# A two-layer transformer kernel on one core: the second half of a decayed attention by way of a state, and a causal mask moved from the matrix engine to the vector engine

## The reference

```
# first attention: 16 heads of 128, 4 key/value heads, rotary, no softmax
lam  = 2 ** (-8 * (1..16) / 16)
o[i] = sum over j <= i of  exp(-lam * (i - j)) * (q[i] . k[j]) * v[j]
# second attention: 32 heads of 16, 8 key/value heads, rotary
scores = q @ k.T / sqrt(16) + triu(-inf, k=1);  y = softmax(scores) @ v
```

## Time and profile before

| | |
|---|---|
| median of 3 runs | 4115.63 us (4114.98 to 4118.08) |
| profiled execution, own time | 4116.67 us |
| its span, first to last instruction | 4114.9 us |
| mean granted TensorE clock | 0.967 of 2.4 GHz |
| PE, DVE, ACT, POOL busy | 3815.0, 2393.4, 1449.7, 1332.2 us |

### The profile page before, as it was taken

How to read it: one execution, slowest core, us unless ns; L and a number is a source line. 1 busy time by engine, 2 the same in 40 slices (tenths; PEclk the granted TensorE clock), 3 DMA queues, 4 the chain that set the end, 5 groups by cost and what they waited for, 6 DMA issues and landing times. The chain is left out here.

```text
span 4114.9 us, 51894 instructions
## 1 busy us (share of the span) xinstructions
PE 3815.0 (93%) x19048; PEld 2746.2 (67%) x19048; DVE 2393.4 (58%) x3950; ACT 1449.7 (35%) x2205; POOL 1332.2 (32%) x1674
## 2 busy tenths in 40 slices
PE   6877999999999999999999999999999999978678
PEld 5755777677767776677767776677767776664423
DVE  5644556555654666556654666456654665465347
ACT  4422342424243433424242433334242433314124
POOL 2421452235312541235313541244213541121114
PEclk9989999999999999999999999999999999987789
DMA  6456533254424433254324533354324433332304
GB/s 234 171 186 245 189 133 139 83 196 158 144 68 179 164 133 127 86 215 147 129 88 154 181 116 135 105 202 138 123 98 180 164 126 105 113 105 73 133 12 153
DMA packets 173802, 579.03 MB, mean 141 GB/s; under 512 B 14728, under 2 KB 14984, under 8 KB 168175
## 3 DMA queue, kind: packets, MB, share of 16 engines
q1 hardware_dynamic: 169854, 568.37, 38.8%
q10 hardware_dynamic: 3696, 7.34, 0.5%
HBM read 490.19 MB, written 84.93 MB: 140 GB/s over the span
## 5 line engine op out<-in xcount | busy, mean ns | idle before, releaser
L1776 PE MATMUL ps_P<-XnT_hi,w_ring 128*128 128x512 f32 x3328 | 1079.6, 406 | 51.6 <-DVE silu L1445 25.7
L1776 PEld LDWEIGHTS ps_P<-XnT_hi,w_ring 128*128 128x128 f32 x3328 | 610.0, 191 | 215.2 <-issue 76.2
L1776 PE MATMUL ps_P<-XnT_lo,w_ring 128*128 128x512 f32 x1664 | 659.0, 396 | 0.0
L1435 DVE TENSOR_REDUCE row_max<-ps_T 128x2 fp32r<-128x768 f32 (+3 forms) x448 | 399.3, 915 | 248.8 <-PE ps_T L1932 238.7
L833 POOL TENSOR_TENSOR pT_lo<-pf,pT_hi 128x512 fp32r<-128x512 f32 x320 | 410.8, 1291 | 303.7 <-ACT pT_hi L971 299.2
L1085 ACT ACTIVATE probs<-ps_E 128x1024 f32<-128x1024 f32 x320 | 327.1, 1022 | 393.2 <-PE ps_E L1947 393.2
L909 POOL TENSOR_TENSOR hT_lo<-hf,hT_hi 128x512 fp32r<-128x512 f32 x128 | 164.3, 1284 | 921.1 <-ACT hT_hi L971 921.1
L851 POOL TENSOR_SCALAR_AFFINE_SELECT probs<-probs 128x512 f32<-128x512 f32 x256 | 159.5, 635 | 652.1 <-ACT probs L1085 651.1
L1776 PEld LDWEIGHTS ps_P<-XnT_lo,w_ring 128*128 128x128 f32 x1664 | 317.6, 191 | 71.4
L1776 PE MATMUL ps_Y<-w_big,hT_hi 128*128 128x512 f32 x896 | 331.5, 416 | 23.0 <-POOL hT_lo L909 11.0
L824 POOL TENSOR_TENSOR sines<-swapped,sinT 128x512 f32<-128x512 f32 x160 | 213.2, 1332 | 348.7 <-ACT swapped L971 342.8
(11 more groups left out here) (307 smaller groups left out, 7263.5 us busy)
## 6 DMA issues: line engine op xcount, KB each, us to landing
w_ring<-split_dram SPq DMA_DIRECT2D x412, 512.0 KB, 3.4
w_big<-split_dram SPq DMA_DIRECT2D x64, 2048.0 KB, 7.8
dec<-decay SPq DMA_DIRECT2D x32, 1024.0 KB, 4.9
split_dram<-w_ring SPq DMA_DIRECT2D x58, 512.0 KB, 4.3
split_dram<-w_big SPq DMA_DIRECT2D x36, 512.0 KB, 4.4
wo1w<-split_dram SPq DMA_DIRECT2D x8, 2048.0 KB, 7.5
gatew<-split_dram SPq DMA_DIRECT2D x7, 2048.0 KB, 10.9
x_dram<-X SPq DMA_DIRECT2D x8, 1024.0 KB, 5.4
```

The source lines that it names most:

```text
L1435: last = dve.reduce_max(row_max[:, g % 2, block, heads_of(ns)].rearrange("p (b n) -> p b n", n=len(ns)), psT[:, :, at:at + len(ns) * w].re ...
L1776: last = pe.matmul(dst, stat[s_], mov[m_], start=first_ and k == 0, stop=last_ and k == n - 1)
```

## The change

In the first attention the sequence is cut in two halves of 256 tokens. Within each half, scores are made as before (three jobs of 512 columns in place of three blocks; the whole square between first and second half is gone). What the first half gives to the second goes by way of a state: keys are turned back to rows (`keys_back`, 4 matmuls of 128 columns), values of the first half are multiplied by their decay (DVE), `state` = keys x these values (6 matmuls of 512 columns), and `state_product` = state x queries of the second half (12 matmuls of 256 columns); DVE multiplies by a decay and adds it to the values' product of the second half. The ring has 10 jobs of ACT and POOL as before, but two of them are now the halves of `oT`. DVE's and ACT's order in the blocks is new.

`keys_back` writes bank Y0, which ACT empties after `swap` of the last unit and `rope_high` of the one before it; the same bank is the target of `output` 0 (and, for g = 0, of `all_values` 0).

In the second attention the two mask matmuls of each `scores` are left out. DVE adds the mask to the corner of the T banks, in place, and waits for its own sum before it takes the maxima. The copies `QT` (second half) and `yT` go from DVE to ACT. The weight pieces of pass 0 are staged in other buffers and split at other places of the blocks.

```diff
+P_F = {k: n for n, k in enumerate((0, 1, 2, 3, 4, 5, "state", 6, 7, 8, 9, "sum0", "sum1"))}
+P_HI = {k: n for n, k in enumerate((0, 1, 2, 3, "state", 4, 5, 6, 7, 8, 9))}
+UNIT_AT, KEYS_AT = (0, 1, 2, 3, 5), 4
@@ POOL blocks: 8 jobs pT_lo, then two that write oT_lo of the second half
@@ ACT rope
+                act.wait_ge(*proj.need(n, g, KEYS_AT))
+                copy(kv[0][:, :], ps["Y0"][:, :]).then_inc(*rope_hi.hit(n, g, KEYS_AT))
                 rope_high(n, g, NU - 1)
@@ ACT blocks
+                for k in range(NJOB):
+                    if k == 4:
+                        act.wait_ge(*pv.need(n, g, 1))
+                        copy(kv[0][:, :], ps[PB[g % 2]][:, :]).then_inc(*p_hi.hit(n, g, P_HI["state"]))
+                    if k == 6 and g == 0:
+                        values_high(n, 2)
+                        values_high(n, 3)
+                    if k == 7:
...
+                        act.wait_ge(*pv.need(n, g, 4))
+                        for h in range(2):
+                            copy(oT[0][:, 2 * h:2 * h + 2, 0:2 * P], ps[EB[h]][:, :]...)
+                    (then copy pT_hi for k < 8, oT_hi of the second half for k = 8, 9)
@@ ACT, second attention
-                copy(QT[:, g % 3, 0, :], ps[bank][:, :]).then_inc(*QT0_done.hit(c, g))
+                for pair, done in enumerate((QT0_done, QT1_done)):
+                    act.wait_ge(*pack.need(c, g, pair))
+                    copy(QT[:, g % 3, pair, :], ps[banks[pair]][:, :]).then_inc(*done.hit(c, g))
+                    copy(yT[:, g % 2, :], ps["O"][:, :]).then_inc(*yT_done.hit(c, g))
@@ DVE blocks
+                for k in range(2):
+                    if g == 0:
+                        values_low(n, k)
+                    scaled_values(n, g, k)
+                if g:
+                    accumulate(n, g - 1, 0)
+                    accumulate(n, g - 1, 1)
+                dve.wait_ge(*dec_in.need(n, g))
+                for k in range(2, 6):
+                    scaled_scores(n, g, k)
+                    if g == 1 and n:
+                        measure_pc(n - 1, k - 2)
+                dve.wait_ge(*p_hi.need(n, g, P_HI["state"]))
+                low(kv[1][:, :], ps[PB[g % 2]][:, :], kv[0][:, :])
+                (accumulate or values_low 2, 3; scaled_scores 6, 7; oT_lo of the first half, twice;
+                 scaled_scores 8, 9; for each half of the heads, after pv 7: pf = ps_E + pf)
@@ DVE, second attention
-                dve.tensor_copy(QT[:, g % 3, 1, :], ps[bank][:, :]).then_inc(*QT1_done.hit(c, g))
-                    dve.tensor_copy(yT[:, g % 2, :], ps["O"][:, :]).then_inc(*yT_done.hit(c, g))
+                    dve.tensor_tensor(corner, corner, mask[:, :]..., ALU.add).then_inc(*corner_done.hit(c, g, x_))
+                    dve.wait_ge(*corner_done.need(c, g, x_))
@@ PE
+            def keys_back(n, g):          # called after project(n, g, 3)
+                pe.wait_ge(*rope_lo.need(n, g, 0))
+                dst = fill("Y0", rope_hi.need(n, g, KEYS_AT))
+                for t in range(2):
+                    for s_ in range(2):
+                        last = pe.matmul(dst[:, cols(2 * t + s_)], kT[s_][:, cols(t)], identr[:, :], start=True, stop=True)
+            def blocks(n, g):
+                for k in range(2, 6):
+                    score_product(n, g, k)
+                if g == 0:
+                    all_values(n, 2)
+                state(n, g)
+                if g == 0:
+                    all_values(n, 3)
+                else:
+                    output(n, g - 1, 2)
+                    output(n, g - 1, 3)
+                value_product(n, g, 2)
+                value_product(n, g, 3)
+                score_product(n, g, 6)
+                score_product(n, g, 7)
+                value_product(n, g, 4)
+                for k in INTER:           # 8, 9
+                    state_product(n, g, k)
+                for k in range(5, 8):
+                    value_product(n, g, k)
@@ PE scores
-                for q in range(2):
-                    last = pe.matmul(corner..., ident_b[:, :], mask[:, :]..., start=False, stop=True)
```

More of the change, by code:

```diff
@@ L61 @@
 RAW = 4
-WO_AT = {2: 2, 5: 3}
 PHASES = [("pre", 0, "T"), ("pre", 0, "agg")]
@@ L175 @@
 assert len(PIECES) == NUNITS == len(set(PIECES))
+MOVED = sum(len(at) for key, at in FIRST.items() if key[0] != "slot")
 INDEX = {p: r for r, p in enumerate(PIECES)}
@@ L1054, in layout_high @@
+                        copy(oT[0][:, 2 * h:2 * h + 2, 2 * P:4 * P], pf[:, k % 2, :].rearrange("p (h i) -> p h i", h=2))\
+                            .then_inc(*p_hi.hit(n, g, P_HI[k]))
+                    if n == 0 and k >= 6:
+                        first(("blk", g, k - 6))
             def layout_high(c, g):
@@ L1110, in _ @@
                                 gate(d)
[L1111 to L1113 removed]
+                            for t in range(2):
+                                values_high(n, t)
                         blocks(n, g)
@@ new lines, in blocks @@
+                low(kv[1][:, :], ps[PB[g % 2]][:, :], kv[0][:, :]).then_inc(*p_f.hit(n, g, P_F["state"]))
+                for t in range(2, NT):
+                    if g:
+                        accumulate(n, g - 1, t)
+                    else:
+                        values_low(n, t)
+                for k in (6, 7):
+                    scaled_scores(n, g, k)
+                    if n == 0 and k == 6:
+                        first(("blk", g, 0))
+                for h in range(2):
+                    dve.wait_ge(*o_hi.need(n, g, h))
+                    low(oT[1][:, 2 * h:2 * h + 2, 0:2 * P], ps[EB[h]][:, :].rearrange("p (h i) -> p h i", h=2),
+                        oT[0][:, 2 * h:2 * h + 2, 0:2 * P]).then_inc(*o_lo.hit(n, g, h))
@@ L1831, in blocks, with state_product @@
+            def state_product(n, g, k):
+                if k == INTER[0]:
+                    pe.wait_ge(*p_f.need(n, g, P_F["state"]))
+                dst = fill(TB[k % 2], p_f.need(n, g, P_F[k]))
+                for m in range(2):
+                    h = 2 * (k - NRING) + m
+                    last = product(dst[:, 2 * m * P:2 * (m + 1) * P], [(halves(kv, cols(h)), halves(qT, h, slice(2 * P, 4 * P)))])
+                last.then_inc(*score.hit(n, g, k - 2))
             def blocks(n, g):
@@ L1920, in scores @@
                 dst = fill_both(TB, max_done.need(c, g, x_))
-                for part, (block, ns, at) in enumerate(STEPS1[x_]):
+                for block, ns, at in STEPS1[x_]:
                     w = (block + 1) * P
```

292 lines of the change are left out of this document (168 added, 124 removed).

## The result

The changed kernel takes 4180.65 us (median, 4177.36 to 4182.68) against 4116.85 of the kernel before in the same comparison: 1.0155 times as long, 95% interval 1.0137 to 1.0172. It is slower by 64 us, where 31 less were forecast; the profiled span went from 4114.9 to 4177.6 us.

The account below looks back on a forecast made before the run. PE was taken to bound both stages, with pass 8 waiting for DVE's maxima. First stage -7.5, second stage -20 over passes 1 to 7, pass 8 -3: -30.5 us, 4085; forecast band 4065 to 4106 (0.42), range 4035 to 4135.

Parts of the forecast that it names:

- the price of the new first attention in groups 1 to 3: First attention: a group goes from 40.2 to 40.3 us, 2.0 us of PE work saved but waits up from 2.1 to 4.2.
- The length of the wait: First attention: PE waits 2.8 us before output 0 for ACT to empty bank Y0 of the turned keys.
- as a rival it had 0.03: First stage: groups' clock falls to 0.92 behind the 2.8 us waits, 3.2 us more x 21 = +67, 4152; chance 0.03.
- POOL's list: First attention blocks: POOL's last job ends 4 us after the last value product, so outputs 2 and 3 wait for nothing.
- Group 0: First attention: two value projections moved into the blocks give POOL time, ending 1.2 us earlier than 55.5; 6 x -1.2 = -7.
- far ahead of need: DMAs of the first attention: SP waits for the state product's use of table `dec`, far ahead of need; no cost put.
- Pass 0: First stage: moved weight splits take about 2 us from three groups, last splits before output 0 of group 3 +2: -4.
- The second attention: Saved 10.9 us per pass, given back 8.0: net -2.9, -20 over passes 1 to 7; pass 8 -3.
- the step from x0 to x1: Second attention: x1 starts 3.15 us after x0, nothing saved, in half of the groups; 1.7 us per pass given back.
- From x1 to x2: Second attention: 0.14 us lost in five groups, 0.3 to 0.7 slower in three; 3.0 us per pass given back.
- The rival that DVE's sum costs time: Second attention: sum PSUM to PSUM takes 1.21 us instead of 0.69, giving +33, 4149; decides from about 1.0 us; chance 0.13.
- the rival of 0.04: Both stages: DVE's sum hidden and the first stage's 2.0 us per group (64 us) come through as well, 3967; chance 0.04.

Follow-up runs that it names:

- the run with the value projections first: Changed kernel with all four value projections of group 0 ahead of the blocks, where the change had moved two into them: 4146.34 us.
- the run with the rstds moved: Changed kernel with POOL's four rstd pairs of pc taken from the end of group 1's blocks to behind the sines of group 2: 4142.63 us.
- four edits: Changed kernel with turned keys in T0, scaled values in the rotation, rstds behind group 2's rotation, all value projections ahead of group 0's blocks: 4101.67 us.
- POOL's jobs last: Kernel with all four of those edits, POOL's low halves of the scaled values put behind the sines of units 3 and 4, not 2 and 3: 4071.59 us.
- keys in T0: Changed kernel with turned keys in bank T0 instead of Y0, except in the first group of passes 2 to 7: 4168.3 us.
- the last kernel: Against POOL's jobs last: DVE's scaled values ahead of the first rotation, POOL's low halves behind the rotation, ACT's group 0 copies between value projections: 4033.88 us.
- middle wait: Kernel before, output 0 of groups 1 to 3 also waiting for ACT's high half of the fourth unit: +75 us.
- long wait: Kernel before, output 0 of groups 1 to 3 also waiting for DVE's low half of the fourth unit: +120 us.
- short wait: Kernel before, output 0 of groups 1 to 3 also waiting for the swap of the last projection: +30 us.
- early values alone: Changed kernel with turned keys in T0 and, in groups 1 to 3, both jobs of scaled values made during the rotation: 4126.05 us.

## Why the prediction was wrong

**The step that failed** is the price of the new first attention in groups 1 to 3, "+0.1 x 21 groups = +2 us"; measured over the 21 groups it was +58. The length of the wait was right (2.8 forecast, 2.59 measured), so was its place, and the blocks behind it took 18.3 us (1920.29 to the next projection at 1938.59) where 17.9 were worked out. Where the clock held, the group came out nearly as the sum had it: group 1 of the run with the value projections first took 40.7 us against 40.8 before, group 2 of the run with the rstds moved 40.0 against 40.2, each with the wait in it. Two things were missing.

First the clock. The sum put it at nothing, and as a rival it had 0.03, for which no reason was given. Its price there, 3.2 us a group, was too high, its chance far too low: behind 22 of 24 waits it fell, 1.6 us each, 35 us. The runs with the wait alone show that PE's idleness does this, with the old work. "Against 1.00 elsewhere" in the prediction was read from three stretches. The kernel before has a wait of 2.3 us itself, at the start of each second stage, and at three of the seven in passes 1 to 7 the clock fell. Timeline of pass 4, PE, and the window of the lower clock:

```profile
2021.25 1.19 PE L1776 MATMUL ps_P<-XnT_hi,w_ring 128*128 128x512 f32 x2 [2.30 <-DVE silu L1445]
2022.24 0.63 PE L1776 MATMUL ps_P<-XnT_lo,w_ring 128*128 128x512 f32 x1
2022.67 1.05 PE L1776 MATMUL ps_P<-XnT_hi,w_ring 128*128 128x512 f32 x2
```
```profile
2020.93:2024.35 3.42, 3.10 (x7) 2.48 (x8) 1.46 (x4) 0.66 (x2) 1.27 (x1) 0.50 1.00 393
```

So the sign of it stood in the trace that the prediction was made from.

Second, POOL: the prediction said of POOL's list only that its last job ends 4 us after the last value product, and that outputs 2 and 3 wait for nothing. It did not ask what is queued behind that job in group 1. It was the four rstds, and group 2 cost 6 us.

**Group 0** was forecast 1.2 us shorter. In the changed kernel it is 1 to 4 us longer, because the table is not "far ahead of need" there: the sentence held for groups 1 to 3 alone. Over passes 2 to 7, -7 became +9. With the table there in time it took 54.3 us, which is the forecast 1.2 less than 55.5, but by chance: that holds a fall of the clock, and the runs with four edits and with POOL's jobs last show the same group at 52.7 where the clock holds. The saving was sized too low and the clock took the rest back.

**Pass 0**: forecast -4, measured +11. PE waits 6.68 us for `w_big` ahead of output 0 of group 3, where +2 had been put for the last splits, and the waits for Y0 are 3.11 us there. With the keys in T0 6.6 us of the 11 go, and the last kernel's first stage there takes 228.3 us against 234.1 before; how the rest splits was not taken apart.

**The second attention** was right in its mechanism: forecast -20 and -3 in pass 8, 23 in all, against 22.8 measured alone. PE's idle pieces in the second stage of pass 2 grew by 7.8 us (7.4 to 15.2) where 8.0 were to be given back. But the step from x0 to x1 of 3.18 us (3.15 forecast) came in two of the eight groups of a pass, not in half of them; four take 2.66, and the first two take 0.7 more than before. From x1 to x2 the first three groups are 0.3 to 0.7 us slower, as forecast, while the other five lose nothing, where 0.14 was put. So that the total fits so well is in part luck, and the clock had a part in it too. Where the clock holds throughout, a second stage goes from 247.6 to 243.8 us, 3.8 less where 2.9 were forecast; over passes 1 to 6 the clock fell five times in this run and three times before, at 1.6 to 1.7 us each, which leaves 3.2 a pass. Inside the changed kernel, with seven falls, it gave 1.9 to 4.0 a pass. The 3.0 us that the forecast gave back for x1 to x2 are also more than its own parts make (5 x 0.14 and 3 x 0.3 to 0.7, 1.6 to 2.8). The rival that DVE's sum costs time fell with the 0.69 us; it needed 1.0. Of the copies on ACT one wait of 0.40 us shows, PE for `QT`.

**The other direction**: the rival of 0.04 had DVE's sum hidden and the first stage's 64 us come through, 3967. The second half of it is near to what the last kernel shows (62 us), but only with the lists rewritten; the first half did not come.

**Left open**: why the clock holds behind some waits of 2.0 us and falls behind others of the same length; how the 64 us split between the three places exactly, since each edit also changed how often the clock fell behind the waits that were left (24 waits: 22, 17 and 15 falls with the rstds and the value projections moved); and pass 0.

## What to carry to other kernels

A new wait on TensorE in the middle of dense work is to be priced at more than its length: here 1.36 us cost itself, and 1.9 to 3.8 us mostly cost another 1.6 us or so (in one kernel in 2 of 13 cases, in others in half to all). Look for waits of that length in the trace at hand, and at the clock behind them. When jobs move to the end of an engine's list, read what is behind them in that list in each pass and each group, not in a typical one: both POOL's rstds and the decay table sat in one group of four. Do not take a single edit's gain for the price of what it removed: it may hold clock falls gained or lost elsewhere. A wait that is removed shows the next one; only when POOL, DVE and the bank were all moved did the saving of the matrix work appear.

## What the runs showed of the hardware

- The granted clock fell to 1.2 GHz, for 3.4 us and sometimes 6.8, at pieces of idleness within otherwise full work: of 1.90 us 21 times of 21 (keys in T0, with 0.44 us more right behind it), of 2.0 to 2.2 us 13 of 24 (middle wait), of 2.6 to 3.1 us 22 of 24 (changed kernel), of 3.3 to 3.8 us 18 of 24 (long wait). It did not fall behind 24 waits of 1.36 us (short wait) nor behind 20 of 1.60 us (POOL's jobs last), and behind two of 7 of 1.8 to 1.9 us (last kernel, group 2). Length alone does not decide: of 2.2 us ahead of the blocks it was 19 of 20 with four edits and 2 of 13 with early values alone.
- DVE's sum with both operands in SBUF took 0.68 us alone and 1.77 us when a POOL product or difference was already running; with one operand in PSUM (`cosine`, 1902.45 in the kernel with POOL's jobs last) it stayed at 0.68 us beside one. Where POOL's sine started with DVE's sum or just behind it, DVE's stayed at 0.68 and POOL's took 1.5 to 1.8 us in place of 1.29. The Trainium skill, "SBUF — State Buffer", section "SBUF: two separate sides", says that the two share a pair of ports under an exclusive lock, which DVE needs with two SBUF inputs; the rows agree.
- DVE can read and write the same PSUM bank at the price of a copy (0.68 us): 0.69 us for 512 elements, 0.43 for 256.
